# ScalarE's order in one block of a two-layer cross-attention, and four scratch tensors in place of two

## What is computed

```python
# layer 0: one head
qn, kvn = layer_norm(x), layer_norm(ctx)
q, k, v = qn @ Wq.T + bq, kvn @ Wk.T + bk, kvn @ Wv.T + bv
x = x + (softmax(q @ k.T) @ v) @ Wd.T + bd
# layer 1: H = 8 heads of D = 256, context of 192 columns
Q, K, V = x @ Wq, ctx @ Wk, ctx @ Wv
attn = softmax(where(mask, Q @ K.T / sqrt(D), -inf))
out = layer_norm((attn @ V) @ Wo + x)
```

## Time and profile before

| | before |
|---|---|
| median of three runs | 511.05 us (510.51 to 511.43) |
| the profiled execution's own time | 510.73 us |
| its span | 508.9 us |
| PE busy | 475.9 us, 94% of the span |
| DVE, ACT, POOL busy | 333.3, 291.6, 244.1 us |
| PE's share of the chain that ended last | 72% |

### The profile page before, as it was taken

The page is one execution under the profiler, slowest core; times in us unless marked ns, Lnnn a source line. Parts: engine busy times, 40 slices in busy tenths (PEclk is TensorE's granted clock), DMA queues, the critical chain, the costliest instruction groups (busy, mean ns, idle before and its releaser), DMA issues.

```text
span 508.9 us, 7590 instructions
## 1 busy us (share of the span) xinstructions
PE 475.9 (94%) x2424; PEld 394.5 (78%) x2424; DVE 333.3 (65%) x681; ACT 291.6 (57%) x480; POOL 244.1 (48%) x151
## 2 busy tenths in 40 slices
PE   0989999999979999999999999999999999999992
PEld 0877787777868888888888888888888888788891
DVE  5999866566565658565756585667656765755467
ACT  4667377466565656666556565666556564656222
POOL 4636664455845353637271727263635453353004
PEclk9999999999999999999999999999999999999997
DMA  8413013757756576465656474747484745561002
GB/s 265 137 44 124 1 47 106 235 163 236 229 168 217 176 205 206 166 207 165 206 165 225 146 222 150 243 140 246 141 254 142 236 150 181 167 204 43 0 2 82
DMA packets 53974, 81.97 MB, mean 161 GB/s; under 512 B 5792, under 2 KB 43072, under 8 KB 53824
## 3 DMA queue, kind: packets, MB, share of 16 engines
q1 hardware_dynamic: 44992, 50.16, 34.3%
q10 hardware_dynamic: 8960, 31.54, 16.5%
HBM read 49.16 MB, written 32.51 MB: 160 GB/s over the span
## 4 chain that ended last, share of the span: by engine, by line
PE 72%; DVE 10%; DMA 7%; ACT 5%; issue 2%; POOL 1%; SPq 1%; DVEq 0%; ACTq 0%; POOLq 0%
PE ps_scores L611 25%; PE ps_o L634 6%; PE ps_o L635 5%; PE ps_o L638 5%; PE ps_o L637 5%; PE ps_o L636 5%; DMA probs_t_lo<-scratch 3%; DMA scratch<-probs 3%; PE ps_task L561 2%; PE ps_task L560 2%; PE ps_task L559 2%; PE ps_out L559 2%; DMA ctx_raw<-in_context 2%; ACT probs L975 1%; PE ps_out L561 1%
## 5 line engine op out<-in xcount | busy, mean ns | idle before, releaser
L506 POOL TENSOR_TENSOR probs_t_lo<-probs_t_lo,probs_t_hi 128x1024 fp32r<-128x1024 f32 (+1 forms) x75 | 146.2, 1960 | 180.6 <-ACT probs_t_hi L987 180.4
L987 ACT ACTIVATE probs_t_hi<-probs_t_lo 128x1024 fp32r<-128x1024 f32 (+1 forms) x75 | 64.6, 881 | 44.3 <-DMA probs_t_lo<-scratch 44.2
L634 PE MATMUL ps_o<-probs_t_hi,val_hi 128*128 128x512 f32 (+1 forms) x144 | 56.6, 393 | 2.8 <-DVE o_lo L1356 2.6
L1301 DVE RECIPROCAL row_inv<-row_sum 128x1 f32<-128x1 f32 x72 | 11.4, 160 | 70.6 <-PE ps_scores L611 68.6
L635 PE MATMUL ps_o<-probs_t_lo,val_hi 128*128 128x512 f32 (+1 forms) x144 | 56.6, 393 | 0.0
L638 PE MATMUL ps_o<-probs_t_lo,val_rem 128*128 128x512 f32 (+1 forms) x144 | 56.4, 391 | 0.0
L637 PE MATMUL ps_o<-probs_t_hi,val_rem 128*128 128x512 f32 (+1 forms) x144 | 56.0, 389 | 0.0
L636 PE MATMUL ps_o<-probs_t_hi,val_lo 128*128 128x512 f32 (+1 forms) x144 | 55.9, 388 | 0.0
L1338 DVE STREAM_TRANSPOSE probs<-probs 128x1024 f32<-128x1024 f32 x30 | 37.4, 1245 | 24.8 <-ACT probs L975 24.8
L611 PE MATMUL ps_scores<-key_hi,q_hi 128*128 128x512 f32 x144 | 46.6, 405 | 2.2 <-DVE neg_scores L1314 1.7
L1338 DVE STREAM_TRANSPOSE neg_scores<-neg_scores 128x1024 f32<-128x1024 f32 x30 | 37.2, 1242 | 14.4 <-ACT neg_scores L975 14.4
(11 more groups left out here) (247 smaller groups left out, 1090.3 us busy)
## 6 DMA issues: line engine op xcount, KB each, us to landing
probs_t_lo<-scratch SPq DMA_DIRECT2D x240, 128.0 KB, 3.0
scratch<-neg_scores ACTq DMA_DIRECT2D x30, 512.0 KB, 3.3
scratch<-probs ACTq DMA_DIRECT2D x30, 512.0 KB, 3.8
ring<-in_weights_a SPq DMA_DIRECT2D x9, 512.0 KB, 5.2
ring<-in_weights_b SPq DMA_DIRECT2D x9, 512.0 KB, 6.0
ring<-in_keys_t SPq DMA_DIRECT2D x4, 512.0 KB, 3.4
ctx_raw<-in_context SPq DMA_DIRECT2D x2, 768.0 KB, 9.1
ring<-in_context SPq DMA_DIRECT2D x16, 96.0 KB, 2.7
```

The costliest lines, as they stand in the source:

```text
L506: nc.gpsimd.tensor_tensor(pt_lo[b][:, t, k, :], pt_lo[b][:, t, k, :].bitcast(f32), moved_part(j, k).bitcast(f32), ALU.subtract).then_inc(m ...
L634: pe.matmul(o0, val_hi[b][:, kt, :], hi, start=first, stop=False)
L987: act.activation(moved_part(j, k), pt_lo[b][:, t, k, :].bitcast(f32), ACT.Copy)\
```

## The change

There are two parts. First, each of a batch's four blocks has a scratch tensor of its own, with semaphores of its own: (h, j) uses number j % 4, where it used j % 2. The wait of `spill` is then for the fetch four blocks back and no longer for the one two blocks back, and DVE's wait names the semaphore of the block two back. Second, ACT's head 1 is written out as `body(1)`, and its loop runs over heads 2 to 6. With h a plain 1, `late` is true in block 1: `round_moved(0, 7)` moves from ahead of the task's rounding to behind `round_outputs(0, 0)`.

```diff
-        scratch = [nc.dram_tensor(f"scratch{i}", [P, KEYS], f32) for i in range(2)]
+        scratch = [nc.dram_tensor(f"scratch{i}", [P, KEYS], f32) for i in range(QT)]
...
-        spilled = [sem(f"spilled{i}") for i in range(2)]
-        fetched = [sem(f"fetched{i}") for i in range(2)]
+        spilled = [sem(f"spilled{i}") for i in range(QT)]
+        fetched = [sem(f"fetched{i}") for i in range(QT)]
...
                 r, b = slots1(h, j), j // QT
-                sp.wait_ge(spilled[j % 2], 64 * h + (16 * (j // 2) + 16))
+                sp.wait_ge(spilled[j % QT], 32 * h + (16 * (j // QT) + 16))
...
-                src = scratch[j % 2][:, :].rearrange("(a p) (n c) -> n p a c", a=4, n=4)
+                src = scratch[j % QT][:, :].rearrange("(a p) (n c) -> n p a c", a=4, n=4)
...
-                    sp.dma_start(dst, src[n]).then_inc(fetched[j % 2], 16)
+                    sp.dma_start(dst, src[n]).then_inc(fetched[j % QT], 16)
...
-                act.wait_ge(fetched[j % 2], 256 * h + (64 * (j // 2) + 64))
+                act.wait_ge(fetched[j % QT], 128 * h + (64 * (j // QT) + 64))
...
-                if not (isinstance(h, int) and r < 2):
-                    act.wait_ge(fetched[j % 2], 256 * h + 64 * (j // 2))
-                act.dma_start(scratch[j % 2][:, :], tiles[j % 2][:, :]).then_inc(spilled[j % 2], 16)
+                if not (isinstance(h, int) and r < QT):
+                    act.wait_ge(fetched[j % QT], 128 * h + 64 * (j // QT))
+                act.dma_start(scratch[j % QT][:, :], tiles[j % 2][:, :]).then_inc(spilled[j % QT], 16)
...
             first_body()
-            with act.Fori(1, HEADS - 1) as h:
+            body(1)
+            with act.Fori(2, HEADS - 1) as h:
                 body(h)
...
-                    dve.wait_ge(spilled[j % 2], 64 * h + 16 * (j // 2))
+                    dve.wait_ge(spilled[(j + 2) % QT], 32 * h + 16 * ((j + 2) // QT))
```

## The result

| | before | after |
|---|---|---|
| median | 511.12 us (510.0 to 513.83, 7 runs) | 508.63 us (507.62 to 509.4, 7 runs) |
| ratio to before | | 0.9935, interval 0.9911 to 0.9959 |
| profiled execution, its span | 510.73, 508.9 us | 507.62, 505.8 us |
| PE busy, share of the span | 475.9 us, 94% | 475.5 us, 94% |
| PE's share of the chain | 72% | 82% |

The change made the kernel faster by 0.65%. The same kernel, measured against before twice more, on two chips, gave 0.9943 and 0.9950, which would be 508.1 and 508.5 us.

What follows compares the result with a forecast made beforehand. PE was taken to bound the kernel, stalled in head 1 by ACT's order. Outputs ahead 2.2 us, scratch tensors 0 and written-out code 0 gave 511.05 - 2.2 = 508.8 us, range 507.8 to 510.2.

Steps and rivals of the forecast that it cites:

- PE bounds, and behind head 1's middle its own work sets the time.: PE, busy 29.96 of 30 us from 160 to 190 us, sets the time; earlier gains reach the end.
- The wait goes back to the order of ACT.: Block 2 of head 1: PE's waits, 3.14 us, come from ready work queued behind L987, where ACT idles 4.10 us.
- the rival that the order is not what holds PE: Head 1: fetched (0, 7) lands behind 142.4 beside two other fetches, each us beyond costing one; chance 0.04.
- The size of the stall's cut, 2.2 us.: Block 2 of head 1: PE starts the values at 144.48 instead of 146.66 us.
- What is late next is the fetched block's own rounding.: Block 2 of head 1: PE waits about 1.0 us for POOL's first half of (0, 7), done at 144.34.
- The transfer of (1, 1) at about 143.5.: ACT in head 1: this transfer is issued at about 143.5 in place of 145.38 us.
- Four scratch tensors: 0, bounds 0 to 1.1.: Transfer of (0, 7) can start 1.1 us earlier, but its landing has slack: taken as 0, bounds 0 to 1.1 us.
- Written-out code: 0.: Writing head 1 out takes register instructions, some 0.04 us each, off ACT where it idles: gain 0.
- The rival of code loading: ACT's moved loop jumps to a target that must be loaded, up to 10.5 us slower, 519.4; chance 0.05.
- Late fetches give the gain back.: Rival: a late landing of (1, 3) in head 1's block 5 makes PE wait in block 6, 509.8 to 510.9; chance 0.12.
- a sign of being wrong: In the profile after, landings of L996 above 3.5 us as a median would show the forecast wrong.
- The clock is 1.00, the higher level of 2.4 GHz, in both stretches, and stays out of the sum.: PE from 130 to 190 us: granted clock at its higher level, so no clock term in the sum.

Runs made afterwards that it cites:

- the order alone: Kernel before with head 1 written out on ACT and outputs ahead of the fetched block, two scratch tensors: mean 508.57 us, ratio 0.9951.
- the finer order: First half of (0, 7) rounded between the outputs, fetched block behind the exponential in other blocks 1 and 5: mean 507.74 us with four scratch tensors, 508.21 with two.
- `s4_half_between`: The change with the first half of (0, 7) rounded between o_hi and o_lo, the second behind them, four scratch tensors: mean 508.46 us, ratio 0.9918.
- the filled kernels: Kernel before with eleven unread 512-column matmuls in PE's two waits in block 2 of head 1, run twice: ratios 0.9993 and 1.0008.
- the loop-order kernel: Kernel before with only the fetched block's rounding moved behind the exponential in blocks 1 and 5 of heads 1 to 7: mean 510.04 us, ratio 0.9958.
- `b2_before_look`: One of two further traces of the unchanged kernel before; the two measured 512.05 and 512.39 us.
- `b3_before_look`: The other of the two further traces of the unchanged kernel before; the two measured 512.05 and 512.39 us.

## Why the prediction was right and where not

- **PE bounds, and behind head 1's middle its own work sets the time.** Right: the window from 160 us is full, and what was gained stayed. In the order alone 0.52 us of it went in block 6.
- **The wait goes back to the order of ACT.** Right. The order alone gives 0.9951, the change 0.9943 on the same chip; the rival that the order is not what holds PE is out.
- **The size of the stall's cut, 2.2 us.** Right against the trace it was worked out from: 2.17. PE's remaining wait was to be 0.8 to 1.0 us and is 0.91; POOL was to end at 144.34 and ended at 144.30; L1015 came at 140.50 (forecast 140.65), L987 at 142.23 (142.37).
- **What is late next is the fetched block's own rounding.** Right. Moving its first half up brought PE's restart 0.73 us forward, with POOL still its releaser after 0.18 us of wait.
- **The transfer of (1, 1) at about 143.5.** Wrong: it was issued at 141.25. I had put it behind L1017 and L987, as it stands in ACT's order. But in the old order too it was issued at 145.38 while L1017 ran (145.21 to 145.80). Both times that is 0.02 to 0.04 us behind the end of DVE's turn (145.36 and 141.21). So ACT's roundings keep their order, but the issue of a transfer is not held by those ahead of it. Nothing in the sum hung on it.
- **Four scratch tensors: 0, bounds 0 to 1.1.** Right: 1.0001 alone, and 0.16 us between the two kernels with outputs ahead. The start came 1.3 us earlier (130.65 after) as said, but the write took up the head start. With the finer order the restart came 0.40 us later with two tensors than with four, in one trace each, on different chips: whether they matter there is open.
- **Written-out code: 0.** Right: 1.0008 for the kernel with nothing else changed. The rival of code loading is out, for there are 11 packets of instructions as before. (The stretch shown has five register instructions on ACT, not six; nothing hangs on it.) The Trainium skill's page "Runtime: NRT & Kernel Launch", section on instruction fetch mechanics, would have made it pay only if the loop's start lay outside the two prefetched lines. No run here shows such a reload.
- **Late fetches give the gain back.** In the three traces of the change they did not. Its landings of L996 have a median of 3.4 us and a maximum of 4.4 in the first, where the earlier trace rows had 3.5 and 5.5. In the two others the median is 3.6, above the 3.5 that had been named a sign of being wrong, and PE lost nothing by it, so that sign was badly chosen. The mechanism is real, though. PE waited in block 6, where this rival had placed it, for 0.52 us with the order alone, 0.7 in `s4_half_between`, and 2.4 and 1.9 in the filled kernels.
- **"The clock is 1.00, the higher level of 2.4 GHz, in both stretches, and stays out of the sum."** This is the step that failed: a term put at nothing. It read one execution whose clock did not fall. Over half of the others have a lower mean clock, and in the two of them that were traced with a fall, the fall behind this stall costs 1.5 us each. The change takes that away as well, 0.7 us on average over the four traces, and 0.9 to 1.1 by the executions sorted by clock. The lower end of the range, the 3.14 us of idle time given back, had the same gap: PE is shown busy while the clock is low, so that time is in no wait. The Trainium skill, in "TensorE: Matmul & The Clock Gate", under why this matters for your kernels, warns of idle gaps between bursts of matmuls; the traces agree that PE had idled just ahead of each fall (2.00 to 2.04 us), and show besides that the same gap of 2.03 us had no fall behind it in the first trace.
- A smaller fault beside it: the stall of 3.14 us was taken for a fixed length. In four traces it is 1.7 us longer than after on average, and 0.8 to 2.8 from one to the next. In the sum the errors cancelled in part, by luck: the stall's mean cut is 1.7 where 2.2 was taken, and 0.7 of clock and 0.25 in block 6 were left out, so the forecast cut is about 0.5 us too small. The interval of the first ratio, 506.5 to 509.0 us, holds the forecast 508.8 and the lower end of the range alike, and the two later ratios give times inside the range. So it is the traces and not the miss by 0.1 us that show the step to be wrong.

What stays open: why filling the stall slows the write of (1, 3), so that the price of the clock is known from the traces' second row and from executions sorted by clock, and not from a kernel that differs in the clock alone; and the spread of the loop-order kernel.

## What to carry to other kernels

On an engine that works in order, put the instruction that waits for a transfer behind the work that is ready, and look for every place with the same pattern: cured at one place it gave 0.5 to 0.65%, and a finer order there with the cure in all other blocks another 0.9 us (507.7, the best mean here). Starting the transfer sooner is no substitute: here the write took longer by what it was given. A wait for a transfer has no fixed length, so take two or three profiles before pricing one from a single row. And when an idle time of PE of 2 to 3 us goes, look at the granted clock behind it in several executions: the fall costs time in which PE is shown busy, and one quiet trace does not show that it never happens.

## What the runs showed of the hardware

- A round trip through HBM by way of four fetches landed between 139.90 and 142.32 us for the same block in different executions and kernels. Its write took 3.2 to 4.2 us when issued at 132.0 to 133.0, and 4.4 to 5.1 when issued at 130.5 to 131.7.
- ACT issued a transfer within 0.04 us of the event that it waited for, at 141.25, ahead of L1017 and L987 that stand before it in ACT's order and started at 141.62 and 142.23.
- At PE's wait of 2.00 to 2.04 us for the outputs the clock fell in three of four traces (`b2_before_look`, `b3_before_look` and the scratch tensors alone, not the first trace), at one of 2.36 us in block 6 of the filled kernel too, and at those of 1.69, 1.79 and 1.91 us not. It went to the lower level of 1.2 GHz: for over 6 us with the scratch tensors alone, at a price of 2.4 us, and for 3 to 4 us in the other three, at 1.5 us each. It began inside the wait with the scratch tensors alone, and 0.6 to 1.4 us behind PE's restart in `b2_before_look` and `b3_before_look` (by windows of 1 us).
- With 11 unneeded matmuls in the gaps the clock was below 0.992 in 2 of 23 executions, instead of 27 of 47 of the kernel before on the same chips.
